# One-hots of the last 16 steps of a graph attention layer: from ScalarE's two passes to GpSimd's one instruction per tile

## The reference, cut to what matters

```
u = leaky_relu(xl[src_f] + xr[dst_f] + e, 0.2)
logits = einsum('ehd,hd->eh', u, att)
p = exp(logits - segment_max(logits, dst_f)[dst_f])
alpha = p / segment_sum(p, dst_f)[dst_f]
msg = xl[src_f] * alpha[:, :, None]
out = segment_sum(msg, dst_f).reshape(n, 128) + bias
```

## Time and profile before

| | us |
|---|---|
| median of 3 runs | 2451.69 (2450.14 to 2454.43) |
| the profiled execution's own time | 2457.53 |
| its span | 2455.4 |
| last gather starts | 2283.50 |
| last aggregation starts | 2357.84 |
| final part starts | 2360.05 |

### The profile page before, as it was taken

The page is one execution under the profiler, slowest core; times in us unless marked ns, Lnnn a source line. Parts: engine busy times, 40 slices in busy tenths (PEclk is TensorE's granted clock), DMA queues, the critical chain, the costliest instruction groups (busy, mean ns, idle before and its releaser), DMA issues. The chain is left out here.

```text
span 2455.4 us, 70077 instructions
## 1 busy us (share of the span) xinstructions
PE 2271.9 (93%) x16556; PEld 1733.2 (71%) x16557; DVE 1498.6 (61%) x4174; ACT 1418.2 (58%) x4331; POOL 1722.7 (70%) x1914
## 2 busy tenths in 40 slices
PE   3968999999999999999999999999999999999977
PEld 2745777767777777777777777777777777777756
DVE  4734666656665666566656665666566656666666
ACT  2714666656665666566656665666566656666643
POOL 3777777777777777777777777777777777777101
PEclk9979999999999999999999999999999999999989
DMA  6244444444444444444444444444444444444027
GB/s 197 81 112 92 104 103 98 99 98 106 98 98 100 105 99 98 100 105 99 98 100 105 99 98 101 104 99 96 102 105 98 98 102 105 98 97 98 22 53 120
DMA packets 288519, 244.84 MB, mean 100 GB/s; under 512 B 168503, under 2 KB 259608, under 8 KB 287826
## 3 DMA queue, kind: packets, MB, share of 16 engines
q1 hardware_dynamic: 221726, 116.00, 21.6%
q0 software_dynamic: 60704, 120.20, 20.7%
q10 hardware_dynamic: 5652, 3.68, 0.5%
HBM read 228.23 MB, written 19.40 MB: 101 GB/s over the span
## 5 line engine op out<-in xcount | busy, mean ns | idle before, releaser
L778 POOL DMA_INDIRECT xl_g<-xl_table,src_tab x1708 | 1637.6, 959 | 522.9 <-issue 515.0
L996 DVE SCALAR_TENSOR_TENSOR uT<-banks,relu 128x256 f32<-128x256 f32 x854 | 348.1, 423 | 496.9 <-issue 474.3
L859 PE MATMUL banks<-msg,onehot 128*128 128x177 f32 x3416 | 634.0, 328 | 7.0 <-DVE acc L975 4.4
L859 PEld LDWEIGHTS banks<-msg,onehot 128*128 128x128 f32 x3416 | 517.9, 191 | 171.7 <-issue 169.1
L909 ACT ACTIVATE relu<-banks 128x256 f32<-128x256 f32 x854 | 318.4, 382 | 512.7 <-PE banks L804 471.3
L897 ACT ACTIVATE distance<-iota_n,minus_slot 128x128 f32<-128x128 f32 x1708 | 541.3, 392 | 0.5
L804 PE MATMUL banks<-ident,xl_g 128*128 128x128 f32 x3416 | 502.9, 291 | 16.5 <-DMA xl_g<-xl_table,src_tab 16.3
L975 DVE TENSOR_TENSOR acc<-acc,banks 128x177 f32 x854 | 289.7, 339 | 334.1 <-PE banks L859 224.0
L804 PEld LDWEIGHTS banks<-ident,xl_g 128*128 128x128 f32 x3416 | 420.6, 194 | 70.6 <-DMA xl_g<-xl_table,src_tab 20.5
L794 PE MATMUL banks<-onehotT,xr_parts 128*128 128x256 bf16 x2562 | 358.1, 276 | 35.0 <-issue 21.1
L902 ACT ACTIVATE onehot<-distance 128x512 f32<-128x512 f32 x427 | 268.9, 630 | 106.0 <-PE banks L859 94.5
(11 more groups left out here) (192 smaller groups left out, 1517.1 us busy)
## 6 DMA issues: line engine op xcount, KB each, us to landing
slot_bc<-slot_dram SPq DMA_DIRECT2D x427, 128.0 KB
xl_g<-xl_table,src_tab POOLq DMA_INDIRECT x1708
rbf<-in_edge_attr SPq DMA_DIRECT2D x854, 32.0 KB
masks<-masks_dram SPq DMA_DIRECT2D x864, 12.1 KB
out<-in_x SPq DMA_DIRECT2D x16, 336.0 KB
out<-result POOLq DMA_DIRECT2D x6, 896.0 KB, 9.6
xl_table<-lr_sb SPq DMA_DIRECT2D x49, 64.0 KB, 1.5
xl_in<-xl_table SPq DMA_DIRECT2D x7, 448.0 KB, 5.0
```

Source lines behind the costliest of these rows:

```text
L778: pool.indirect_dma_start(out=xl_g[:, k % RING, t], out_offset=None, in_=xl_table, in_offset=bass.IndirectOffsetOnAxis(ap=src_tab[:, e:e + ...
L859: mm = nc.tensor.matmul(U_ps[h], onehot[:, j % 2, t], msg[:, j % 2, t], start=i == 0, stop=i == PT - 1)
L996: nc.vector.scalar_tensor_tensor(out=uT[:, s % 2, h * PIECE:(h + 1) * PIECE], in0=z_ps[h], scalar=SLOPE, in1=relu[:, h], op0=ALU.mult, op1 ...
```

## The change

For the last 16 steps (411 to 426, from `DRAIN` on) ACT no longer makes distances and one-hots. POOL makes them behind its last gather: for each tile one instruction that adds the tile's column of minus_slot to the column numbers and compares the sum with 0. POOL waits for the aggregation of step m - 2, as ACT's relu did, and before the first also for ACT's last one-hots. PE waits for POOL's semaphore in those steps. ACT's copy of the attributes, which was ordered behind the relu's wait, gets that wait for itself.

```diff
+        DRAIN = STEPS - LAG + 1
...
+            for m in range(DRAIN, STEPS):
+                pool.wait_ge(agg_done, TICK * (m - 1))
+                if m == DRAIN:
+                    pool.wait_ge(oh_ready, TICK * DRAIN)
+                for t in range(TILES):
+                    nc.gpsimd.tensor_scalar(onehot[:, m % 2, t], iota_n[:], minus_slot[:, one(TILES * m + t)], 0.0,
+                                            ALU.add, ALU.is_equal).then_inc(drain_ready, 1)
...
-                    pe.wait_ge(oh_ready, TICK * (k - LAG + 1))
+                    if isinstance(k, int) and k - LAG >= DRAIN:
+                        pe.wait_ge(drain_ready, TILES * (k - LAG - DRAIN + 1))
+                    else:
+                        pe.wait_ge(oh_ready, TICK * (k - LAG + 1))
...
-                if inside(k - LAG + 1, STEPS):
+                if inside(k - LAG + 1, DRAIN):
...
                 if inside(k - LAG + 1, STEPS):
+                    if isinstance(k, int) and k - LAG + 1 >= DRAIN:
+                        act.wait_ge(agg_done, TICK * (k - LAG))
                     nc.scalar.activation(msg[:, m % 2, :, CNT:AGG].rearrange("p (i h) k -> p i h k", i=PT),
```

More of the change, by code:

```diff
@@ L712, in edge_loop @@
          ends_listed, fall_ready, shrink_ready, back_done, ends_ready, firsts_raised, run_ready, below_ready,
-         last_ready, weight_ready, wT_done, spread_done, factor_ready, rescaled, x_set) = map(sem, (
+         last_ready, weight_ready, wT_done, spread_done, factor_ready, rescaled, x_set, drain_ready) = map(sem, (
              "set_up", "acc_zero", "ohT_ready", "node_saved", "rbfT_done", "rbfT_ready", "z_done", "relu_ready", "u_ready", "L_done",
@@ L717, in edge_loop @@
              "back_done", "ends_ready", "firsts_raised", "run_ready", "below_ready", "last_ready", "weight_ready",
-             "wT_done", "spread_done", "factor_ready", "rescaled", "x_set"))
+             "wT_done", "spread_done", "factor_ready", "rescaled", "x_set", "drain_ready"))
         XPARTS = 16
         XPART = (FBATCH - 1) * FB * P // XPARTS
+        DRAIN = STEPS - LAG + 1
         block = ctx.enter_context(nc.Block())
```

## The result

The changed kernel takes 2462.56 us (median of 6 runs, 2454.39 to 2468.47), the kernel before 2452.03 in the same comparison (6 runs, 2450.13 to 2459.07). The ratio is 1.0033, with a 95% interval of 1.0019 to 1.0048, which is 4.7 to 11.8 us. The forecast was 2451.5 us and no change, with 2447.5 to 2459.5 as its range.

A forecast was written before the change was run, and what follows sets the result against it. The prediction saw no engine busy throughout the 48.15 us drain, only steps waiting for one another. A gain of 0.9 us at its end and 0.7 us lost on DVE gave -0.2 on 2451.69, so 2451.5 us; range 2447.5 to 2459.5.

The forecast's parts named there:

- From the last aggregation's start to the final part it is 2360.05 - 2357.84 = 2.21 us, unchanged: End of the drain: the stretch behind the last aggregation was to keep its 2.21 us, adding nothing to the forecast.
- T: Time of one POOL one-hot instruction in the drain, taken as 0.53 us, with bounds of 292 ns and 928 ns.
- The prediction's own threshold: In rival 1: from T = 0.69 us on, POOL bounds the whole drain, as 2313.5 + 64T passes 2357.84.
- rival 1: POOL in the drain too slow, T above 0.64 us, kernel slower, up to 2466.8 us; chance 0.22.
- The end's formula, 5.1 - 8T: Last steps of the drain: gain if POOL starts step 425's one-hots when step 423's aggregation ends; 0.9 us.
- POOL beside DVE: Nine two-input DVE instructions on the batches' chains in the drain each lengthen by 0.075 us beside POOL; 0.7 us lost.
- Rival 2: In the drain POOL and DVE block each other fully, 2.4 us lost in place of 0.7, giving 2453.2 us; chance 0.13.
- Rival 3: POOL fast in the drain, T at 0.35 us or less, ceiling gain of 2.1 us, giving 2449.9 us; chance 0.10.
- The wait added before ACT's attribute copy: On ACT in the drain: the copy's own wait for the aggregation two steps back was to cost 0.

The follow-up runs named there:

- late clearing: Kernel before, plus one tiny POOL instruction clearing 8 columns of an unused tile after the aggregation of step 425; ratio 1.0028 (1.0016 to 1.0041).
- one-operation kernel: Changed kernel with POOL's instruction only comparing minus_slot with a tile of negative column numbers, one operation in place of two; ratio 1.0036 (1.0023 to 1.0049).
- kernel without gathers: Kernel of the late clearing, but SyncE fills the 24 row buffers once with plain copies and all steps use those; one execution, 2470 us.
- 96 gathers: Kernel of the late clearing, but POOL gathers for the first 24 steps only and later steps use those rows again; one execution, 2544 us.
- second comparison: Repeated timing of early distances against the kernel before, on a chip where the latter took 3633 us; ratio 1.0015 (0.9982 to 1.0047).
- early distances: Kernel before, without POOL's one-hots: in the drain ACT computes the next step's distances right behind its attribute copy; ratios 0.9969, 1.0015 and 0.9993 in three comparisons.
- third comparison: Last timing of early distances against the kernel before: 2452.81 against 2454.26 us, ratio 0.9993 (0.9983 to 1.0004).

## Why the prediction was wrong

The prediction read right what bounds the drain before, that POOL's gathers are out of the way, and how few steps wait for ACT. The step that failed is the sentence "From the last aggregation's start to the final part it is 2360.05 - 2357.84 = 2.21 us, unchanged". I took these 2.21 us as a chain of PE and DVE that the change doesn't touch. But the block's end is a wait for all engines, POOL among them, and POOL's way to it was 8.2 us long and hidden. The trace of the kernel before held the answer: POOL's idle time before the final part ends with the queue's own record of line 663, not with the end of a gather:

```profile
2360.05 0.52 POOL L1132 MEMSET mean<- 128x512 f32 x1 [75.26 <-POOLq L663]
```

I read that idle time as room, since the profile doesn't count drains as work, and looked at no line's queue records. The late clearing, with all one-hots left on ACT, puts most of that price on the kernel: the gap is 8.00 us in place of 2.21.

The second failure is the size of T: 0.69 us in place of 0.53. I halved line 368's variable part. But with one operation the 128-wide instruction takes 0.60 us and the 256-wide 0.928, so the fixed part (with the conversion left aside) is 0.27 us and not 0.19, and the second operation, to which I gave nothing, is 0.11. The prediction's own threshold then speaks: from 0.69 on POOL bounds the whole drain. By pace alone it would just have been in time, 2313.5 + 64 x 0.692 = 2357.8 against 2357.84. It was 2.2 us late, by what the formula left out: 1.1 us by which six instructions were lengthened beside DVE (below), 0.9 us in which POOL waited for a free buffer (0.64 of it before step 412), and 0.25 us from POOL's last one-hot to the aggregation where I had put 0.1; the rest is below 0.1 us. So rival 1 came, at its mild end, and would alone have been within what can't be told from no change. The end's formula, 5.1 - 8T, had no test: in both kernels with 16 steps on POOL it was behind long before step 425 (with one operation its last 20 instructions ran without a wait), so it was never the end of step 423's aggregation that released it.

**POOL beside DVE** was given 0.7 us, all of it on DVE. On the chains DVE lost half of that: the scan of line 1011 went from 679 to 777 ns, lines 1035 and 1039 from 476 and 485 to 515 and 570 on average, twice each, and the short scans stayed at 696 and 695, together 0.35 us. What the sum left out is that POOL's instructions become longer too. The seventh of the 64 took 1.06 us; it started at 2312.95, inside the first of the two short scans (rows of the changed kernel):

```profile
2312.26 1.75 POOL L788 TENSOR_SCALAR onehot<-iota_n,minus_slot 128x128 f32<-128x128 f32 x2
2312.79 0.70 DVE L1033 TENSOR_TENSOR_SCAN seq_forth<-seq_cut,seq_in 1x264 f32<-1x264 f32 x1
...
2313.52 0.69 DVE L1036 TENSOR_TENSOR_SCAN seq_max<-seq_cut,seq_forth 1x264 f32<-1x264 f32 x1
```

Two undisturbed ones take 1.40 us, this pair 1.75. Each of the six long ones lies beside a DVE instruction with two inputs in SBUF (the short scans of both batches, lines 1049 and 1065), and since POOL bounds the drain, their 1.1 us count in full. In the one-operation kernel POOL was first, in both batches: in the first its instruction started at 2316.77, the scan just behind it, and now the scan took 0.84 us in place of 0.70:

```profile
2316.77 0.60 POOL L791 TENSOR_SCALAR onehot<-minus_iota,minus_slot 128x128 f32<-128x128 f32 x1
2316.85 0.84 DVE L1036 TENSOR_TENSOR_SCAN seq_forth<-seq_cut,seq_in 1x264 f32<-1x264 f32 x1
```

By the Trainium skill (SBUF — State Buffer, "Who interferes with whom") such a pair contends, and the issue order decides who blocks. These two places agree. That the later one fully blocks, which the same section says of VectorE's 2-port modes and the prediction took for this pair, doesn't show here: 0.54 us of the first scan were left when POOL's instruction started, and POOL lost 0.35; the second scan started inside that instruction and lost nothing. Rival 2 thus had the right pair, but neither the size nor the engine that pays: it put 2.4 us on DVE, and the runs show 0.35 there and 1.1 on POOL.

Rival 3 fell with T at 0.69 us, over twice the select's 0.29. The Trainium skill (GPSIMD Engine Reference, "Engine selection") calls one-input operations roughly line rate; this instruction is not, with 0.58 us for 128 elements, 4.5 ns an element, in its one-operation form. The wait added before ACT's attribute copy cost nothing visible: PE's last releasers in the drain are POOL and DVE, not that copy.

The range failed because its upper side was built from T alone, and the larger price was a term that stood at zero. On the shown median of 2451.69 us the tail's 6.0 us alone give 2457.7, inside the range, and with the 2.2 us 2459.9, just above its end of 2459.5.

## What to carry to other kernels

An engine that "has nothing more to do" in a block still has its way out of it, and a job added at the block's end moves that way out into the open. Before work is put on an idle engine near a barrier, read how long after its last work that engine's drain ended, above all on GpSimd when it has issued gathers, and let the new work end earlier than the others by at least that much. A price taken from a row of half the fit (one operation, other width) needs a bound for each difference, most of all where a threshold lies close by. When GpSimd becomes the bound, look at how its own instructions grow beside VectorE's, not only at the reverse. And before a microsecond between two traces is called a gain, see how far traces of the same schedule lie apart and at what granted clock each ran.

## What the runs showed of the hardware

- POOL's drain at the end of the edge loop ends behind POOL's last work by 0.1 us without gathers in that block, 0.7 with 8, 7.9 with 96 and 8.2 with 1708. With 1708 it is 8.2 us whether the last gather lies 0 or 75 us back, and with 96 it is 7.9 after 2190 us. Behind six plain transfers issued by POOL (the final part) it is 7.3 us.
- POOL's tensor-scalar instruction on 128x128 32-bit floats with a column operand: one every 0.58 us with one operation, every 0.69 with two. Beside DVE instructions with two inputs in SBUF single ones took 0.81 to 1.06 us (two operations) and up to 0.98 (one), and in turn a 1x264 scan on DVE took 0.84 us in place of 0.70.
- The kernel before took 3636 and 3633 us on two chips, at a mean granted clock near 0.85, and 2452 to 2456 in the other comparisons at 0.98. On these two chips the kernel without gathers took 2470 us at 0.97 and that with 96 gathers 2544 at 0.96, one execution each. So the extra time comes with the gathers; which part of a gather is slow isn't shown, for POOL's own instruction for one took 952 ns there (second comparison, early distances) and 958 in the third. In a middle stretch of 200 us of the early-distance kernel PE was busy 144 us there at a granted clock of 0.86, and 192 us at 0.98 in the third comparison.
